# A six-layer local-attention stack on one core: the order of transposes, scores and values products, a squared guess on ScalarE, and one operation less on GpSimd

## The reference

```python
def attn_layer(x, Wqkv, qs, ksc, Wo):            # 16 heads of 64, DEPTH = 6
    qkv = x @ Wqkv
    q, k, v = jnp.split(qkv, 3, -1)
    ...
    q = l2norm(q) * qs                           # t / max(norm(t), 1e-12)
    k = l2norm(k) * ksc
    ...
    q = q * cos * scale + rotate_half(q) * sin * scale
    k = k * cos * inv + rotate_half(k) * sin * inv
    out = local_attention(q, k, v)               # windows of 32, each sees itself and the one before
    out = out.transpose(0, 2, 1, 3).reshape(b, n, INNER)
    return out @ Wo

for i in range(DEPTH):
    x = attn_layer(shift_tokens(x), Wqkv[i], q_scale[i], k_scale[i], Wo[i]) + x
    x = ffn_layer(shift_tokens(x), ln_g[i], ln_b[i], W1[i], b1[i], W2[i], b2[i]) + x
```

## Time and profile before

| what | value |
|---|---|
| median of 3 runs | 2305.26 us (2302.34 to 2305.34) |
| profiled execution, its own time | 2298.88 us |
| its span, first to last instruction | 2297.1 us |
| mean granted clock of PE | 0.98 |
| busy: PE, DVE, ACT, POOL | 94%, 74%, 68%, 61% |

### The profile page before, as it was taken

The page is one execution under the profiler, slowest core; times in us unless marked ns, Lnnn a source line. Parts: engine busy times, 40 slices in busy tenths (PEclk is TensorE's granted clock), DMA queues, the critical chain, the costliest instruction groups (busy, mean ns, idle before and its releaser), DMA issues.

```text
span 2297.1 us, 104869 instructions
## 1 busy us (share of the span) xinstructions
PE 2163.7 (94%) x36357; PEld 1677.6 (73%) x36357; DVE 1708.3 (74%) x4617; ACT 1555.0 (68%) x5192; POOL 1410.4 (61%) x2639
## 2 busy tenths in 40 slices
PE   6999789998999989999899998999989999899998
PEld 4776267776888758887588875788857888578885
DVE  4777878886888758787578875778757877578874
ACT  3553545554888748887488884888848888478883
POOL 3442711112888728887288882888828888288881
PEclk9997999997999999999999999999999999999999
DMA  3000000001211102111021110311103111021110
GB/s 102 0 0 1 0 1 0 0 0 54 75 41 42 35 26 75 40 42 35 23 77 42 41 36 18 81 42 39 39 18 79 42 40 40 16 51 43 42 40 20
DMA packets 120016, 82.33 MB, mean 36 GB/s; under 512 B 50998, under 2 KB 112580, under 8 KB 119876
## 3 DMA queue, kind: packets, MB, share of 16 engines
q1 hardware_dynamic: 119876, 80.43, 13.5%
HBM read 21.94 MB, written 1.05 MB: 10 GB/s over the span
## 4 chain that ended last, share of the span: by engine, by line
PE 74%; issue 5%; DVE 4%; POOL 2%; ACT 1%; DVEq 0%; POOLq 0%; ACTq 0%
PE bank L818 14%; PE bank L835 9%; PE bank L902 7%; PE bank L882 6%; PE bank L862 6%; PE bank L827 6%; PE bank L892 4%; PE bank L845 4%; PE bank L757 2%; PE bank L854 2%; PE bank L746 2%; PE bank L949 2%; PE bank L948 2%; PE bank L605 2%; PE bank L959 1%
## 5 line engine op out<-in xcount | busy, mean ns | idle before, releaser
L534 POOL TENSOR_TENSOR l_qk<-l_rot 128x512 f32<-128x512 f32 x384 | 494.2, 1287 | 106.0 <-DVE l_rot L1597 58.8
L1593 DVE TENSOR_TENSOR l_rot<-bank,l_tab 128x512 f32<-128x512 f32 x384 | 265.0, 690 | 185.7 <-ACT l_sq L1194 185.1
L1210 ACT ACTIVATE l_qkT<-bank 128x512 f32<-128x512 f32 x384 | 229.6, 598 | 255.2 <-PE bank L835 255.2
L555 POOL TENSOR_TENSOR l_qk<-l_qk,l_rn 128x512 f32<-128x512 f32 x384 | 400.7, 1044 | 0.9
L1174 ACT ACTIVATE prob<-bank,peak 128x64 f32<-128x64 f32 x1536 | 353.9, 321 | 1.3 <-DVE peak L1615 1.3
L818 PE MATMUL bank<-w_high,xs_part 128*128 128x512 f32 x768 | 347.4, 452 | 6.0 <-DVE xs_part L1584 5.4
L1597 DVE TENSOR_TENSOR l_rot<-bank,l_tab 128x512 f32<-128x512 f32 x384 | 261.4, 681 | 0.0
L1607 DVE TENSOR_REDUCE l_ss<-l_sq 128x8 f32<-128x512 f32 x384 | 259.6, 676 | 0.2
L835 PE MATMUL bank<-const,l_qk 128*128 128x128 f32 x1536 | 252.9, 287 | 6.5 <-POOL l_qk L555 5.8
L1194 ACT ACTIVATE l_sq<-bank 128x512 f32<-128x512 f32 x384 | 236.0, 615 | 23.8 <-PE bank L818 16.0
L902 PE MATMUL bank<-l_wo,l_oT 128*128 128x128 f32 x1536 | 237.4, 277 | 0.0
(11 more groups left out here) (201 smaller groups left out, 5287.8 us busy)
## 6 DMA issues: line engine op xcount, KB each, us to landing
stash<-l_v SPq DMA_DIRECT2D x768, 65.0 KB, 2.0
early<-in_L_ffn_Wqkv_dram SPq DMA_DIRECT2D x36, 256.0 KB, 3.1
l_wo<-in_L_ffn_Wo_dram SPq DMA_DIRECT2D x6, 512.0 KB, 4.0
xin<-Y SPq DMA_DIRECT2D x96, 32.0 KB
xin<-Y SPq DMA_DIRECT2D x96, 31.8 KB
f_w<-in_L_ffn_W_dram SPq DMA_DIRECT2D x6, 341.0 KB
out_dram<-X SPq DMA_DIRECT2D x4, 256.0 KB, 2.3
f_w<-in_L_ffn_W_dram SPq DMA_DIRECT2D x6, 128.0 KB
```

Of the source, the lines that this page charges most:

```text
L534: pool.tensor_tensor(l_qk[:, k], l_rot[:, k, 0], l_rot[:, k, 1], ALU.add).then_inc(l["add_done"], 1)
L555: pool.tensor_tensor(v, v, l_rn[:, k, :, None].broadcast_to([128, 8, L_DIM]), ALU.mult).then_inc(l["qk_done"], 1)
L1593: dve.tensor_tensor(l_rot[:, k, 0].rearrange("p (q h n) -> p q h n", q=2, h=4), bank[:, 0, :].rearrange("p (q h n) -> p q h n", q=2, h=4), ...
```

## The change

In the layers' attention alone:

- PE: the transposes of q and k (unit c-4) come first in the slot, then the scores (unit c-5), and behind these the values products (unit c-6). All else keeps its order.
- ACT squares the guess y into a new tile l_yy (skew 3), behind the rounding of x and in front of the evacuation of q and k.
- POOL takes y squared from there: its Newton step has three operations in place of four. It moves from skew 4 in front of the addition to skew 3 behind it, and the multiplication goes to the front of the slot. The queue goes add, factor, multiply for one unit and then for the next; it went factor of u, add of u+1, multiply of u.
- DVE: the residual addition stands behind the rotation products.

```diff
@@ -213,6 +213,7 @@
         l_s = sb("l_s", [128, 2, 8])
         l_rn = sb("l_rn", [128, 2, 8])
         l_y = sb("l_y", [128, 2, 8])
+        l_yy = sb("l_yy", [128, 2, 8])
         l_t = sb("l_t", [128, 8])
         l_qk = sb("l_qk", [128, 2, 512])
 
@@ -265,7 +266,7 @@
                  "x_turned kvT_done v_proj v_done qk_proj rot_done evac_done rope_done o_turned oT_done out_done "
                  "res_done y_copied y_stats y_stat y_pool y_rstd y_done")
         l = stage_sems("l_", core.replace("sub_done ", "") + "w_high_done w_split "
-                 "x_turned x_high_done x_split qk_proj v_proj rot_done sq_done ss_done floored logged guessed newton rn_done "
+                 "x_turned x_high_done x_split qk_proj v_proj rot_done sq_done ss_done floored logged guessed squared newton rn_done "
                  "add_done qk_done qk_turned qkT_done v_done o_turned oT_done out_done res_done")
         f = stage_sems("f_", "xs stats stat pool_st rstd n_done turned nT_done hidden gelu_done h_done out_mm yb_done "
                  "y_done")
@@ -537,14 +538,12 @@
 
                     k = j % 2
                     y, t = l_y[:, k], l_t[:]
-                    pool.wait_ge(l["guessed"], upto(ub, u + 1))
-                    pool.tensor_tensor(t, l_s[:, k], y, ALU.mult).then_inc(l["newton"], 1)
-                    pool.wait_ge(l["newton"], upto(3 * ub, 3 * u + 1))
-                    pool.tensor_tensor(t, t, y, ALU.mult).then_inc(l["newton"], 1)
-                    pool.wait_ge(l["newton"], upto(3 * ub, 3 * u + 2))
+                    pool.wait_ge(l["squared"], upto(ub, u + 1))
+                    pool.tensor_tensor(t, l_s[:, k], l_yy[:, k], ALU.mult).then_inc(l["newton"], 1)
+                    pool.wait_ge(l["newton"], upto(2 * ub, 2 * u + 1))
                     apart(pool)
                     pool.tensor_scalar(t, t, -0.5, 1.5, ALU.mult, ALU.add).then_inc(l["newton"], 1)
-                    pool.wait_ge(l["newton"], upto(3 * ub, 3 * u + 3))
+                    pool.wait_ge(l["newton"], upto(2 * ub, 2 * u + 2))
                     pool.tensor_tensor(l_rn[:, k], t, y, ALU.mult).then_inc(l["rn_done"], 1)
 
                 def l_scale(u, b, j):
@@ -555,7 +554,7 @@
                     pool.tensor_tensor(v, v, l_rn[:, k, :, None].broadcast_to([128, 8, L_DIM]),
                                        ALU.mult).then_inc(l["qk_done"], 1)
 
-                return Pipeline(pool, [(4, l_norm), (3, l_add), (4, l_scale)], UNITS, UNROLL, 4)
+                return Pipeline(pool, [(4, l_scale), (3, l_add), (3, l_norm)], UNITS, UNROLL, 4)
 
             def feed_forward(ly, *groups):
                 fb = ly * 4
@@ -904,7 +903,8 @@
                     if g == 3:
                         ins.then_inc(l["out_done"], 1)
 
-                stages = [(5, l_scores), (4, l_turn_qk), (6, l_pv), (1, l_project_qk), (1, l_project_v), (7, l_output), (6, l_turn_o), (5, l_turn), (0, l_turn_x)]
+                stages = [(4, l_turn_qk), (5, l_scores), (6, l_pv), (1, l_project_qk), (1, l_project_v), (7, l_output),
+                          (6, l_turn_o), (5, l_turn), (0, l_turn_x)]
                 return Pipeline(pe, stages, UNITS, UNROLL, 4)
 
             def feed_forward(ly):
@@ -1204,6 +1204,11 @@
                     act.wait_ge(l["logged"], upto(ub, u + 1))
                     act.activation(l_y[:, k], l_y[:, k], ACT.Exp, scale=-0.5).then_inc(l["guessed"], 1)
 
+                def l_square_guess(u, b, j):
+                    k = j % 2
+                    act.wait_ge(l["guessed"], upto(ub, u + 1))
+                    act.activation(l_yy[:, k], l_y[:, k], ACT.Square).then_inc(l["squared"], 1)
+
                 def l_copy_qk(u, b, j):
                     act.wait_ge(l["qk_turned"], upto(ub, u + 1))
                     act.wait_ge(l["s_done"], upto(ub, u - 1))
@@ -1216,7 +1221,8 @@
                     act.activation(l_oT[:, j // 4, 2 * g:2 * g + 2].rearrange("p a n -> p (a n)"),
                                    bank[:, 6, 0:256], ACT.Copy).then_inc(l["oT_done"], 1)
 
-                return Pipeline(act, [(3, l_log), (2, l_copy_v), (3, l_guess), (7, l_copy_o), (6, l_copy_prob), (1, l_copy_x), (4, l_copy_qk), (5, l_exp), (1, l_square)], UNITS, UNROLL, 4)
+                return Pipeline(act, [(3, l_log), (2, l_copy_v), (3, l_guess), (7, l_copy_o), (6, l_copy_prob), (1, l_copy_x),
+                                      (3, l_square_guess), (4, l_copy_qk), (5, l_exp), (1, l_square)], UNITS, UNROLL, 4)
 
             def feed_forward(ly):
                 fb = ly * 4
@@ -1639,7 +1645,8 @@
                         dve.wait_ge(l["out_done"], upto(bb, b + 1))
                         dve.tensor_tensor(one(Y, b), one(Y, b), bank[:, 7, 256:384], ALU.add).then_inc(l["res_done"], 1)
 
-                return Pipeline(dve, [(1, l_split_x), (5, l_peaks), (2, l_sum_squares), (6, l_divide), (2, l_floor), (7, l_residual), (1, l_rotate)],
+                return Pipeline(dve, [(1, l_split_x), (5, l_peaks), (2, l_sum_squares), (6, l_divide), (2, l_floor), (1, l_rotate),
+                                      (7, l_residual)],
                                 UNITS, UNROLL, 4)
 
             def feed_forward(ly):
```

## The result

| kernel | median us | runs from, to | ratio to before (95%) |
|---|---|---|---|
| before, beside it | 2302.34 | 2298.86 to 2305.34 | 1 |
| after | 2287.01 | 2281.23 to 2289.44 | 0.993 (0.991 to 0.9949) |

The change makes the kernel faster by 15 us, 0.7%. The forecast was 62 us, so the direction holds and the size does not. The profiled execution has a span of 2285.6 us (2297.1 before) at a granted clock of 0.98, as before.

The account below looks back on a forecast made before the run. PE was taken as the bound, its steps between groups setting each slot. Slots 55.7 us plus layer starts 6.4 us, 62.1 off 2298.88, gave 2236.8, as a median 2243 us; own range 2222 to 2270, 8 in 10 2196 to 2288.

Parts of the forecast that it names:

- Transposes 0.15 us cheaper: PE's transposes of q and k, moved from between tiled groups, would take 0.44 us instead of 0.59 to the next group.
- Crossing from scores to products, 0.37 us: On PE, scores (L862) to values products (L882) would take 0.37 us against 0.38, with bounds 0.25 and 0.53.
- L882 to L818 keep their neighbours and their price: On PE, the step from values products to projection would stay at its 0.40 us.
- 0.28 us are left, so it is late by nothing: DVE's division would end at 1008.22, 0.28 us before the transposes of o at 1008.50, so PE would not wait.
- A slot: Each steady slot of the layers would lose 0.16 us, ends 0 and 0.28; over 6 layers x 58 slots 55.7 us.
- Start of a layer, 6.4 us: POOL's first multiplication at a layer's start would end 1.07 us earlier, six times, 6.4 us in all.
- Cover on ACT and POOL: ACT's added square would be hidden; POOL's unit takes 3.30 us, leaving 0.43 us before the transposes of q and k.
- rival 1: Crossing from scores to products is free: 0.28 us saved a slot, 103 us in all, median 2202 us; chance 20%.
- Rival 2: Crossing from scores to products takes 0.53 us, eating the saving; only layer starts gain, 2292 to 2305 us; chance 14%.
- Rival 3: POOL's factor waits for ACT's square, so PE waits at each slot's head: slower, 2334 us; chance 11%.

Follow-up runs that it names:

- experiment 1: Kernel before with the new PE order alone: 2322.06 us, ratio 1.0098; kernel after with the old PE order: 2296.02 us, ratio 0.998.
- before, twice: Kernel before with the values products of r = 0 issued twice, same output: 2426.9 us, ratio 1.0568.
- experiments 2 and 4: Kernel after with products' waits moved before the scores: 2293.07 us; without PE's already covered waits: 2278.09 us; with those left out and moved-values waits early: 2275.23 us.
- experiment 2: Kernel after with the products' waits for o and the moved values taken between transposes and scores: 2293.07 us, ratio 0.9971.
- experiment 3: Two more semaphore instructions in front of the products: in the kernel after 2363.97 us, ratio 1.027; in the kernel before 2335.42 us, ratio 1.0154.

## Why the prediction was off

- **Transposes 0.15 us cheaper:** right, 603 to 447 ns (mean). The row of the layer's start was the right one to price them by.
- **Crossing from scores to products, 0.37 us:** the median is 0.348, the mean 0.424. The value comes in steps, 0.32 to 0.35 us with two semaphore instructions, some 0.445 with a register instruction more, up to 0.65 at the head of the loop. I took one value from the middle of two bounds where the code has four cases; the mean belongs in the sum. Saved 0.01 in my sum, 0.032 lost in the runs.
- **"L882 to L818 keep their neighbours and their price":** the first step that failed. Their neighbour in front had changed, from transposes to 32 other small matmuls. L882 to L818 costs 0.055 us a slot more (0.393 to 0.448), and 0.14 more in the runs where the crossing is free. I priced crossing and products each by itself, where the runs show one floor of 0.643 us under both.
- **"0.28 us are left, so it is late by nothing":** the second step that failed, and the reason why I put the groups behind at nothing. The size was right: the division of DVE (L1638) ends 0.30 us before the transposes of o in the slot shown, 0.29 in the median, where it was 0.68 before. But it is not enough. PE's sequencer waits for the division, and then still has to get to the transposes: in the slot shown the division ends at 1007.20, the wait at 1007.25, and the transposes start at 1007.50. The view of the sequencer's instructions with this wait, in after (ns, min/median/max; the longest was 1262 in before):

```profile
L801 PEldq EVENT_SEMAPHORE  x705: 51/51/1519, 576.4 to 2239.7; - x177
```

In after, the 261 slots in which the division ends 0.2 to 0.3 us ahead have 459, 231 and 260 ns for output, transposes of o and transposes of the probabilities, each to the next group; the 84 slots with 0.3 to 0.45 us have 448, 220 and 223. Together with some slots in which PE waits outright this is the 0.05 to 0.06 us. It comes with the PE order (the new PE order alone: output 510 ns, against 491 in before and in all but the PE order). And it goes where the products come later behind the scores: with two more semaphore instructions and with the products twice the division is 0.49 and 0.47 us ahead, and the output takes 491 and 490 ns again.
- **A slot:** 0.156 saved, 0.032 + 0.055 + some 0.05 given back, 0.02 left where I had 0.16. 348 slots x 0.02 = 7 us in place of 55.7.
- **Start of a layer, 6.4 us:** right in size, some 1.1 us a start from the last matmul of the feed-forward (L959) to the eighth slot (mean of the five layers that have one in front), but in part by luck. I took the whole 1.07 us by which POOL's first multiplication comes earlier, though PE was idle for only 0.25 us before the first transposes. They start 0.41 us sooner behind the feed-forward in three of five layers and no sooner in two; the rest comes in the slots after, the first three of which POOL had paced at 3.35 us; they now take 2.89, 2.96 and 3.50 us, and I had put their gain at nothing. The first multiplication (POOL) now ends at 851.17, before PE is done with the feed-forward, and the transposes don't wait. POOL's and PE's timeline there, which answer to the earlier trace rows:

```profile
849.10 0.20 POOL L542 TENSOR_TENSOR l_t<-l_s,l_yy 128x8 f32<-128x8 f32 x1 [7.28 <-ACT l_yy L1210]
...
850.13 1.04 POOL L554 TENSOR_TENSOR l_qk<-l_qk,l_rn 128x512 f32<-128x512 f32 x1
```

```profile
850.78 1.28 PE L959 MATMUL bank<-f_w,f_h 128*128 128x128 f32 x10
851.89 0.60 PE L834 MATMUL bank<-const,l_qk 128*128 128x128 f32 x4
```

- **Cover on ACT and POOL:** right. The square took 0.21 us, the exponentials start 0.60 us after the products (0.56 forecast), the multiplication ends 0.63 us before the transposes of q and k (0.43), and POOL's own pace is 3.27 us (3.30). Timeline of ACT, DVE and POOL in the slot shown above, which answers to the earlier trace rows:

```profile
1004.94 0.21 ACT L1210 ACTIVATE l_yy<-l_y 128x8 f32<-128x8 f32 x1
...
1005.23 0.20 POOL L542 TENSOR_TENSOR l_t<-l_s,l_yy 128x8 f32<-128x8 f32 x1 [0.29 <-ACT l_yy L1210]
...
1006.10 0.93 ACT L1174 ACTIVATE prob<-bank,peak 128x64 f32<-128x64 f32 x4 [0.45 <-DVE peak L1621]
...
1006.26 1.05 POOL L554 TENSOR_TENSOR l_qk<-l_qk,l_rn 128x512 f32<-128x512 f32 x1
...
1006.78 0.42 DVE L1638 TENSOR_TENSOR o<-bank,rsum 128x256 f32<-128x256 f32 x1
```

- **The rivals:** rival 1 (the crossing is free) was right of the array and wrong of the time: the crossing can be had for 0.27 us and the kernel is then no faster. Rival 2 (what is saved is taken) was nearest, and not by its mechanism: it looked for the loss in the crossing alone, and most of it stands further on, 0.055 in the products and some 0.05 behind them. Rival 3 did not occur with this order of POOL and ACT, and did with the old one (experiment 1).

## What to carry to other kernels

When groups of many small tiled matmuls are put directly behind each other, the drain between them goes, but don't price the second group by what it cost behind a long group. Look for a floor under the two together: here 64 matmuls of 64x32 tiles took 0.64 us from first to last start, where the two groups' own starts take 0.24 and 0.25. Removing waits between the groups then moves the time from the crossing into the second group and gains nothing. Semaphore instructions on TensorE's sequencer cost most in front of such a group (0.10 us each here, net); waits which another wait has already covered are worth leaving out, 7 to 9 us here in either order. And ask of an engine off the path not only whether it is done in time, but by how much: 0.28 us ahead of the transposes was too little, 0.47 was enough.

## What the runs showed of the hardware

- Of 48 products on 64x32 tiles in a row, 32 start within 0.24 us, 7 ns apart in the main, and the 16 behind them take 0.27 us, 17 ns each (before, twice). Two groups of 32 need 0.643 us from first to last start when 0.33 us or less lie between their first starts (after, experiments 2 and 4).
- Between two groups of the same tile size the next matmul can start 0.03 us after the last (experiment 2); between 64x32 and 128x128 it takes 0.15 us.
- A semaphore instruction recorded at 51 ns on PE's sequencer makes the crossing 0.15 us longer, and cost 0.10 us of the kernel's time in the new order and 0.046 in the old (experiment 3).
- An activation on 128x8 takes 0.21 us on ACT, and POOL's chain of three dependent operations on 128x8, with a multiplication on 128x512 behind it, takes 3.27 us with the addition, as forecast from its parts.
